# Attention B: the window of each value product is cut to the columns it needs

## The reference, cut to what matters

```
scores = where(causal, -inf, q @ k.T / sqrt(8))          # within a segment of 64 tokens
A_dot  = softmax(scores) @ v                             # v has 8 columns per head
A_mem  = (sigma(q) @ M) / (sum(sigma(q) * z) + eps)      # memory of the segments before
A_s    = beta * A_mem + (1 - beta) * A_dot
M, z   = M + sigma(k).T @ (v - V_prev), z + sum(sigma(k))
```

## Time and profile before

| | |
|---|---|
| median of three runs | 1736.06 us (1729.93 to 1736.63) |
| the profiled execution, its own time | 1733.57 us |
| span of its core, first to last instruction | 1731.8 us |
| TensorE busy | 1501.8 us, 87% of the span |
| weight loads busy (beside the matmuls) | 1285.4 us, 74% |
| VectorE / ScalarE / GpSimd busy | 1354.8 / 813.1 / 880.2 us |
| mean granted TensorE clock | 0.949 of full |
| L1613, value products of attention B | x1024 records, 176.6 us, mean 297 ns |
| their weight loads | x1024, 141.1 us, mean 199 ns |
| L1379, zeros into the two `vb`, GpSimd | x2, 682 ns each, at 1001 and 1013 us |

### The profile page before, as it was taken

One profiled execution on the slowest core, in us unless ns is written; L12 is line 12 of the kernel. 1 busy time (PEld: TensorE's weight loads), 2 busy tenths in 40 slices (PEclk: granted clock), 3 DMA queues, 4 the chain that ended last, 5 costly groups with the idle time before them and its releaser, 6 DMA issues. The chain is left out here.

```text
span 1731.8 us, 46136 instructions
## 1 busy us (share of the span) xinstructions
PE 1501.8 (87%) x13668; PEld 1285.4 (74%) x13668; DVE 1354.8 (78%) x3426; ACT 813.1 (47%) x1859; POOL 880.2 (51%) x1180
## 2 busy tenths in 40 slices
PE   5999999999999999996687648888888888888887
PEld 4999898998898998995566436666666666666665
DVE  5589999999999999995345366788887877788874
ACT  1556666665665666664466523333333333333331
POOL 4365565665566665654688543333343433333331
PEclk9999999999999999998799868999999999999997
DMA  4432233322222322220444232333333333333330
GB/s 141 142 94 89 78 82 91 91 81 74 81 82 91 91 76 76 80 76 15 136 124 132 58 93 86 96 99 100 98 102 97 101 97 100 98 101 100 94 92 17
DMA packets 181694, 158.10 MB, mean 91 GB/s; under 512 B 12529, under 2 KB 163185, under 8 KB 181618
## 3 DMA queue, kind: packets, MB, share of 16 engines
q1 hardware_dynamic: 181618, 157.17, 31.3%
HBM read 113.09 MB, written 44.04 MB: 91 GB/s over the span
## 5 line engine op out<-in xcount | busy, mean ns | idle before, releaser
L587 PE MATMUL a_bank<-a_vp,a_prob 128*128 128x96 f32 x4096 | 635.2, 261 | 0.0
L587 PEld LDWEIGHTS a_bank<-a_vp,a_prob 128*128 128x128 f32 x4096 | 610.7, 192 | 5.6
L481 ACT ACTIVATE a_prob<-a_bank 128x512 f32<-128x512 f32 x512 | 305.9, 598 | 267.9 <-PE a_bank L571 267.0
L675 DVE TENSOR_REDUCE a_nmax<-a_bank 128x2 f32<-128x512 f32 x512 | 345.1, 680 | 47.7 <-PE a_bank L556 40.7
L556 PE MATMUL a_bank<-a_k_st,a_q_st 96*128 96x256 bf16 x1024 | 259.2, 276 | 36.3 <-DVE a_nmax L675 35.1
L571 PE MATMUL a_bank<-a_q_st,a_k_st 120*128 120x256 bf16 x1024 | 281.7, 276 | 3.2 <-POOL a_q_st L344 3.2
L1613 PE MATMUL c_o_bank<-c_vb,c_prob 128*128 128x96 f32 x1024 | 176.6, 297 | 30.1 <-DVE c_ad L1896 29.3
L344 POOL TENSOR_SCALAR a_q_st<-a_mt 24x2048 bf16<-24x2048 bf16 x64 | 121.4, 1896 | 138.9 <-PE a_bank L571 94.8
L1771 DVE TENSOR_REDUCE c_nmax<-c_bank 128x4 f32<-128x512 f32 x256 | 165.0, 681 | 31.4 <-PE c_bank L1583 29.9
L1487 ACT ACTIVATE c_prob<-c_bank 128x256 f32<-128x256 f32 x256 | 98.8, 386 | 176.2 <-PE c_bank L1563 174.5
L1613 PEld LDWEIGHTS c_o_bank<-c_vb,c_prob 128*128 128x128 f32 x1024 | 141.1, 199 | 41.4 <-DVE c_ad L1896 29.1
(11 more groups left out here) (202 smaller groups left out, 2999.8 us busy)
## 6 DMA issues: line engine op xcount, KB each, us to landing
a_q_st<-scratch_a_parts_dram SPq DMA_DIRECT2D x64, 288.0 KB
a_k_st<-scratch_a_parts_dram SPq DMA_DIRECT2D x192, 96.0 KB
c_q_st<-scratch_c_parts_dram SPq DMA_DIRECT2D x64, 288.0 KB
c_k_st<-scratch_c_parts_dram SPq DMA_DIRECT2D x192, 96.0 KB
scratch_a_parts_dram<-a_parts SPq DMA_DIRECT2D x32, 384.0 KB, 2.7
scratch_c_parts_dram<-c_parts SPq DMA_DIRECT2D x32, 384.0 KB, 2.7
a_x<-in_x SPq DMA_DIRECT2D x32, 128.0 KB, 3.2
scratch_y<-a_y SPq DMA_DIRECT2D x32, 128.0 KB, 2.7
```

Of the source, the lines that this page charges most:

```text
L481: act.activation(prob[h % 4][:, :, :].rearrange("p a b -> p (a b)"), t_ps[h % 2][:, :], ACT.Exp).then_inc(exped, 1)
L587: mm = pe.matmul(o_ps[g % 2][:, at:at + VC], prob[h % 4][:, c, t * P:(t + 1) * P], vp[o][:, c, :], start=c == 0, stop=c == NT - 1)
L675: dve.tensor_reduce(nmax[:, t, 2 * g:2 * g + 2], s_ps[t][:, :].rearrange("p (h k) -> p h k", h=2), AX.X, ALU.max, negate=True).then_inc(ma ...
```

## The change

`WIN` becomes `VP`: each value product reads and writes the 36 columns of its own group. `vb` becomes 36 * 7 + 36 = 288 columns wide in place of 348. Nothing else changes; the number of instructions, their order and all waits stay.

```diff
--- before.py
+++ after.py
@@ -1166,7 +1166,7 @@
         MW = HV + H
         VP = 2 * 2 * (HD + 1)
 
-        WIN = 96
+        WIN = VP
         VW = VP * (H // 2 - 1) + WIN
         BROWS = SEG + NPART * H // 2
         ST = 8
```

## The result

The changed kernel takes 1853.18 us (median of 4 runs, 1847.35 to 1857.3), the kernel before 1736.2 us beside it: 1.0687 times as long [1.0665, 1.0708], so 117 us slower where 42 us were forecast. It is slower, inside the range on record, and nearly three times as far from no change as the forecast said.

The account below looks back on a forecast made before the run. Attention B was taken as bound by TensorE's order of work, with two waits for VectorE an item. Streaming 0, new falls 17.7 us, longer low stretches 22.5 and the end 2 gave +42 us: 1777 us, range 1732 to 1890.

Parts of the forecast that it names:

- The direct part: Value products' streaming in attention B: weight loads set the pace, so removed columns save nothing; bounds 0 and 1.6 us.
- Falls at the item's start: At attention B's item starts, TensorE's 2.32 us of 3.30 drops to 2.12, so the clock newly falls there.
- The price of a low microsecond: Time lost per microsecond at low clock in attention B: 0.43 us for longer stretches, 0.34 in a single short one.
- In each pair, one new fall at an item's start: Attention B, 15.4 pairs of items: one added clock fall each at 1.15 us, 17.7 us in all.
- Of the two low stretches a pair then has, one stays low for 3.4 us more: Attention B, 15.4 pairs: one longer low stretch each, at 0.43 us per low microsecond, 22.5 us in all.
- The clock stays low for long: Rival, attention B: long low stretches as at the trace's end; 1844 us at low share 0.4, 1886 at 0.5; chance 0.23.
- Columns as the price: Rival, value products: columns are paid for in time, 0.05 us saved per record, 51 us in all, 1683 us; chance 0.03.
- The order of L1808: Rival, long items: L1808 and L1427 swap order, removing 0.99 us and the fall behind it 12 times, 1708 us; chance 0.04.
- The clock that takes no notice of columns: Rival, attention B: weight loads may count for the clock as well, so nothing changes, 1732 to 1736 us; chance 0.12.
- Does less than its code says: Rival, product width: 68 columns, so 28 off in place of 60, about half the loss, 1755 us; chance 0.03.
- What the prediction said would show it: Signs: L1613 0.11 to 0.12 us apart, clock near 0.89, falls at item starts, two low lengths, 20.3 us items, L1808 alternating.

Follow-up runs that it names:

- the fillers in the dense part: Changed kernel (36 columns) plus two unneeded 224-column bf16 matmuls before each group of products: 1755.7 us, 1.0088 of the kernel before.
- the order with 96 columns: Kernel before (96 columns), with GpSimd's L1427 made to start only behind VectorE's L1808: 1697.24 us, ratio 0.9756.
- The fillers of 8 columns: Changed kernel plus 14 unneeded 8-column matmuls an item in two places where TensorE waits: 1809.65 us, 1.0421 of the kernel before.
- the wide fillers: 14 unneeded 128-column matmuls an item in TensorE's two waits: added to the changed kernel 1755.79 us, to the kernel before 1714.86 us.
- the changed kernel with it and fillers: Changed kernel with L1427 only behind L1808, plus 14 unneeded 128-column matmuls an item in TensorE's two waits: 1695.22 us, 0.977 of the kernel before.

## Why the prediction was wrong, point by point

- **The direct part** was right: the weight load sets the pace, 0.11 us before and after, and 60 columns are worth nothing at a clock that holds (1695 against 1697 us). The 0.05 us that the last product of a group gives back is taken up by the next matmul (0.75 us for both, where it was 0.74). An item at full clock shows about 0.1 us saved, within the prediction's bounds of 0 and 1.6.
- **Falls at the item's start** were right in their place: it falls where it had held, in four of the six items of the pattern. The number put to them was wrong: busy time was to drop from 2.32 to 2.12 of 3.30 us, and it is still 2.32. The profile's busy time doesn't shrink with the columns, since the loads stay; what fell away is streaming, as the prediction itself said of the low stretches.
- **The price of a low microsecond** was right: 0.40 us, between 0.34 and 0.43.
- **What failed is the number and the length of the low stretches**: "In each pair, one new fall at an item's start" and "Of the two low stretches a pair then has, one stays low for 3.4 us more". By these 15.4 pairs would add 15.4 x 6.8 = 105 low us. The trace has 304 more. New falls there were: 41 stretches in place of 18, 23 more where 15 were expected. Their length is most of the miss: the mean stretch went from 3.6 to 9.0 us. I had let one stretch in two last one step longer. Nothing in the mechanism stops it at one step. At low clock a product's load takes longer, 0.21 us in place of 0.11, so less is streamed in the same time, and the next step can be poor in streaming for the same reason. That this is what keeps the clock low fits the runs and is not shown by itself. What ends a long stretch stays open. Score matmuls alone don't: the stretch from 1326.80 us has them at three places, the last from 1344.99 to 1346.67 us, and the clock came back only at 1350.6 us, with the projections of 256 columns (L1663, L1664) in between. The end of the trace before had shown four such stretches in a row, and I put it into the rival "The clock stays low for long", with 0.23, since scores were missing there. At f = 0.4 that rival gave 1844 us, 9 us below the measured median; the share measured in the windows, 374 / 779 = 0.48, is higher, at a lower price per low microsecond.
- **The rivals on the other side.** Columns as the price (1683 us) fell: L1613 keeps its spacing. The order of L1808 did not turn in the changed kernel; put there by hand it gave 1697 us, where the prediction had 1708 for a thing that didn't happen: right in kind, a gain of 39 us and not 26 to 28. The clock that takes no notice of columns (1732 to 1736 us) fell by the row of widths 128, 96, 68, 36. "Does less than its code says" gave 1755 us for 68 columns; 68 columns measure 1749.83, and the code has 36.
- **What the prediction said would show it**: the spacing of 0.11 us, the alternation of L1808, and falls at item starts are in the trace; a clock near 0.89 and two lengths of low stretch are not: from 1041 us to the end it is 0.75, with lengths up to 23.9 us. Items at 20.3 us are gone from the regular part, since hardly an item is without a fall.

Several expectations of experiments failed. Better than expected came out 68 columns (1750 us for 1760 to 1815), the fillers in the dense part (1756 for 1785) and the order with 96 columns (1697 for 1703 to 1712). The fillers of 8 columns fit neither of their two cases. With the wide fillers the time fitted but the clock in attention B did not: with 36 columns it was 0.92 and not 0.95, and with 96 columns not all falls behind L1808 went.

## What to carry to other kernels

Before cutting streamed columns from a matmul, look at what sets its pace. Behind the weight loads of 128x128 fp32 tiles they were free here up to 128 columns, and taking 60 of them away cost 6.9% through the clock. In a kernel that sits near a fall of the granted clock, price every low stretch by its length as well as its number, with one case in which it doesn't end by itself; then look for the waits that start them: one wait that put GpSimd's instruction behind VectorE's took 2.4% off the kernel before, and the best version of these runs is before with that wait, or the changed kernel with it and fillers.

## What the hardware showed that was not expected

- Added matmuls make the kernel faster: 14 needless ones an item take the changed kernel from 1853 to 1756 us, and the kernel before from 1736 to 1715 us.
- TensorE at its lower clock for over 20 us with 0.40 us of idle time by the profile; what ended it is open.
- Less than 0.1 us decides 0.99 us: with L1427 started 20 ns ahead of L1808 that takes 1.27 us, with L1427 40 ns behind it 0.28 us, and on the long one hangs a fall of the clock and, with 36 columns, stretches of 20 us.
- Fillers of 8 columns win back 44 us, though they stream next to nothing; why is open.
